# Moving the transposes of the next x back by one step in a fused attention and network kernel

## The reference, cut to what matters

```
emb = silu(sin_emb(timestep)) @ W_ada + b_ada
scale, shift = split(emb)
x = ln(src) * (1 + scale) + shift
q, k, v = x @ Wq + bq, x @ Wk + bk, x @ Wv + bv
scores = q k^T / 4 + attention_bias, masked;  probs = softmax(scores)
x = x + (probs v) @ Wo + bo
```

## Time and profile before

| what | value |
|---|---|
| median of 3 runs | 994.39 us (993.97 to 995.47) |
| profiled execution | 993.79 us, its span 992.0 us |
| attention of the 8 samples | from about 34 to 720 us of the span |
| one sample | 83.5 to 84.3 us |
| steps 14 to 17 of samples 1 to 6 | near 142, 226, 310, 393, 478 and 562 us |

### The profile page before, as it was taken

How to read it: one execution, slowest core, us unless ns; L and a number is a source line. 1 busy time by engine, 2 the same in 40 slices (tenths; PEclk the granted TensorE clock), 3 DMA queues, 4 the chain that set the end, 5 groups by cost and what they waited for, 6 DMA issues and landing times. The chain is left out here.

```text
span 992.0 us, 19948 instructions
## 1 busy us (share of the span) xinstructions
PE 928.4 (94%) x5758; PEld 615.4 (62%) x5838; DVE 749.0 (76%) x2000; ACT 690.1 (70%) x1126; POOL 701.3 (71%) x542
## 2 busy tenths in 40 slices
PE   5879989999998999999999899979999999999996
PEld 5646556655655655665565566545577777777574
DVE  7888788878879787887986878788444765677565
ACT  3577888898788798879878888888644444545333
POOL 1788788788878869878886977877554545567465
PEclk9999999999999999999999999999999999999998
DMA  8988988996996899699689779965111110111101
GB/s 289 326 311 299 381 300 284 340 376 219 333 387 253 294 380 346 234 339 383 238 294 390 282 267 343 368 250 207 64 64 43 43 43 22 43 65 43 43 22 64
DMA packets 127533, 229.96 MB, mean 232 GB/s; under 512 B 6512, under 2 KB 53872, under 8 KB 123632
## 3 DMA queue, kind: packets, MB, share of 16 engines
q1 hardware_dynamic: 127472, 229.26, 63.8%
HBM read 187.30 MB, written 41.94 MB: 231 GB/s over the span
## 5 line engine op out<-in xcount | busy, mean ns | idle before, releaser
L938 ACT ACTIVATE prob<-prob,nmax 128x512 f32<-128x512 f32 x512 | 356.6, 728 | 56.7 <-DVE nmax L760 53.9
L760 DVE CUSTOM_DVE_ANT_0 prob<-s_bank,big 128x512 f32<-128x512 f32 x512 | 338.7, 685 | 63.4 <-POOL big L1102 30.3
L1102 POOL TENSOR_TENSOR big<-big,mterm_early 128x2048 f32<-128x2048 f32 (+2 forms) x88 | 305.7, 3488 | 73.9 <-DMA big<-in_fside_Bx16xSxS 57.6
L591 PEld LDWEIGHTS t_bank<-ident,prob 128*128 128x128 f32 x2048 | 239.8, 141 | 167.5 <-issue 51.7
L591 PE MATMUL t_bank<-ident,prob 128*128 128x128 f32 x2048 | 318.6, 278 | 18.3 <-ACT prob L938 7.1
L945 ACT COPY pt<-t_bank 128x512 f32<-128x512 f32 x312 | 181.0, 583 | 55.4 <-PE t_bank L591 54.2
L769 DVE COPY pt<-t_bank 128x512 f32<-128x512 f32 x200 | 137.3, 687 | 40.0 <-PE t_bank L591 39.8
L579 PE MATMUL s_bank<-stack_k,stack_q 128*128 128x512 bf16 x432 | 165.0, 382 | 2.2 <-DVE nmax L760 1.6
L605 PE MATMUL o_bank<-pt,val 128*32 128x512 f32 x1024 | 122.9, 598 | 3.7 <-issue 1.0
L2201 POOL TENSOR_TENSOR gl<-big,gh 128x512 fp32r<-128x512 f32 x64 | 83.0, 1305 | 49.6 <-DVE gh L1743 49.6
L2052 ACT ACTIVATE big<-bank,late 128x512 f32<-128x512 f32 x62 | 42.6, 689 | 72.6 <-PE bank L1450 69.1
(11 more groups left out here) (247 smaller groups left out, 1454.8 us busy)
## 6 DMA issues: line engine op xcount, KB each, us to landing
big<-in_fside_Bx16xSxS SPq DMA_DIRECT2D x128, 1024.0 KB, 8.0
pieces_dram<-pieces SPq DMA_DIRECT2D x64, 384.0 KB, 7.2
stack_q<-pieces_dram SPq DMA_DIRECT2D x15, 1024.0 KB, 7.8
stack_k<-pieces_dram SPq DMA_DIRECT2D x15, 1024.0 KB, 9.7
pieces_dram<-pieces SPq DMA_DIRECT2D x32, 256.0 KB, 7.4
xin<-in_x SPq DMA_DIRECT2D x8, 512.0 KB, 8.6
x_dram<-x SPq DMA_DIRECT2D x8, 512.0 KB, 2.6
x1r<-x_dram SPq DMA_DIRECT2D x8, 512.0 KB, 4.3
```

Source lines behind the costliest of these rows:

```text
L591: last = pe.transpose(t_bank[n % 2][:, c * P:(c + 1) * P], prob[:, n % NT, c * P:(c + 1) * P], ident[:])
L760: dve.tensor_tensor_reduce(out=prob[:, n % NT, :], in0=s_bank[n % 3][:, :], in1=bias[:, h % NB, t, :], scale=-1.0, scalar=3e38, op0=ALU.ad ...
L938: act.activation(tile, tile, ACT.Exp, bias=nmax[:, n % NT:n % NT + 1], scale=-1.0).then_inc(exped.sem, 1)
L1102: pool.tensor_tensor(bias[:, h % NB, tiles], bias[:, h % NB, tiles], mterm[:, tiles], ALU.add).then_inc(masked.sem, 1)
```

## The change

The two entries of XT in AHEAD go from steps 14 and 15 to steps 15 and 16. VectorE's copies of them, which follow the list, go from steps 15 and 16 to 16 and 17. TAIL with the output projections is as it was. The order within the list and the banks that the uses get are the same.

```diff
 TAIL = [("O", 3, 6, 1), ("C", 0, 7, 1), ("C", 1, 9, 1), ("W", 0, 10, 1), ("W", 1, 12, 1)]
-AHEAD = [("XT", 0, 14, 0), ("XT", 1, 15, 0), ("Q", 0, 21, 0), ("K", 0, 23, 0), ("Q", 1, 28, 0), ("K", 1, 29, 0)]
+AHEAD = [("XT", 0, 15, 0), ("XT", 1, 16, 0), ("Q", 0, 21, 0), ("K", 0, 23, 0), ("Q", 1, 28, 0), ("K", 1, 29, 0)]
```

## The result

The changed kernel takes 996.12 us, the median of 22 runs, beside 994.15 us for the kernel before in 22 runs on the same chips. The ratio is 1.0023, with a 95% interval of 1.0013 to 1.0034: slower by 1.3 to 3.4 us. The profiled execution took 996.44 us (span 994.6), 2.65 more than that of before.

What follows compares the result with a forecast made beforehand. TensorE, busy 94% of the span, was taken as the bound. Samples 1 to 5 +1.70 us, sample 6 -1.33, sample 0 and the last 0: +0.37, put on the 994.39 us median gives 994.8; range 993.4 to 996.9.

Steps and rivals of the forecast that it cites:

- The gate: Turn of step 16 waits for VectorE's copy of step 14; XT 1 falls behind it, weighing 0.34 us later per sample.
- That nothing is caught up later: After steps 14 to 17 TensorE waits only 0.2 us in all (313 to 375 us), so any loss there is kept.
- the term of -1.33 in the sum: Sample 6, behind XT 0: the low clock goes as the longest pause shrinks to 0.93 us; weighing 1.33 us earlier.
- the low clock stays: Rival: a low clock remains in sample 6 or another sample; 6 x 0.34 = +2.04 us, 996.4; chance 0.22.
- a fall in every sample: Rival: frequent short idles make the clock fall in each of samples 1 to 6; +10.4 us, 1004.8; chance 0.04.
- No DMA moves: Whole kernel: the change moves no DMA, only eight transposes on TensorE and two VectorE copies per sample, by one step.
- 1.8 us of cover: XT 1's copy on VectorE ends at 314.99, ACT's high parts read it at 316.78; so its delay costs nothing.
- Sample 0: No output projection ahead and TensorE full there, so the swap costs nothing; bounded by 0 and one 0.34 us.
- Filled for good: Rival: scores of step 18 and turn of step 15 fill XT 0's pause, kept; -4.3 us, 990.1; chance 0.07.
- Absorbed: Rival: VectorE's waits for POOL's masked bias swallow the 0.34; only sample 6 counts, about -1.7 us, 992.7; chance 0.09.

Runs made afterwards that it cites:

- xt_15_15: The kernel before with XT 0 and XT 1 both at step 15: 994.8 us, ratio 1.0008 to the kernel before.
- xt_14_16: The kernel before with XT 1 alone moved, to step 16, XT 0 staying at 14: 999.0 us, ratio 1.0051.
- old_guard8: The kernel before, with POOL's mask add of head 8 waiting until VectorE's low parts are done: 994.6 us, ratio 1.0001.
- first_new: The kernel before with XT at steps 15 and 16 in sample 0 alone: 994.91 us, ratio 1.0020.
- new_guard8: The changed kernel, with POOL's mask add of head 8 waiting until VectorE's low parts are done: 995.49 us, ratio 1.0017 to the kernel before.
- first_old: The changed kernel with XT back at steps 14 and 15 in sample 0 alone: 995.97 us, ratio 1.0013 to the kernel before.
- xt_16_17: The kernel before with XT 0 and XT 1 at steps 16 and 17: 1016.17 us, ratio 1.0248.
- new_take14_act: The changed kernel with step 14 out of DVE_TAKES, so ACT copies that turned tile: 994.58 us, ratio 0.9999 to the kernel before.
- first_new_again: Repeated timing of the kernel before with XT at steps 15 and 16 in sample 0 alone: 994.46 us, ratio 1.0002.

## Why the prediction was right, and where it wasn't

**The gate: right, in place and size.** The turn of step 16 starts 1.87 us behind XT 0 (1.86 in the prediction), the pause for L769 is there at 0.78 in the row (0.94 counted from the end of the issue, as the prediction counted its 0.93), the weighing comes 3.10 us after XT 0 (3.10). XT 0 itself waited 0.00 to 0.48 us and not always 0.51, because the normalisation took 2.43 us in sample 3 where the row of before had 2.75. Four things bear it out: xt_15_15 with 2.66 against 2.65 worked out, xt_14_16 with 3.10, the pair with the late terms at step 20, where the 0.34 is 0.35, and the 2.16 us up to the weighing in samples 1 to 6. That nothing is caught up later held too: from 316 to 378 us TensorE waited 0.2 us in all, as in rows 3, and behind the weighing the samples take the same time in both orders.

**The clock: the term of -1.33 in the sum was wrong.** The one low clock behind XT 0 in sample 6 went into the sum as if each execution had it. Three more profiles have the old order in samples 1 to 6 (old_guard8, first_new and its repetition), and there the clock didn't fall behind XT 0 in any of 18 places, not behind pauses of 1.54 us (first_new, sample 4) and 2.24 us (old_guard8, sample 1) either, so the length of the pause, on which the term was built, doesn't decide it; in xt_14_16, with the same pause ahead of XT 0, it fell in two of six. With the old order itself that is one fall in 24 places, about 0.25 an execution at 1.67 us each; with xt_14_16 it is three in 30, about 0.6. So by this estimate 0.4 to 1 us may be won on average, and not 1.67 each time. In the new order (changed, new_guard8, first_old) none of 18 places fell, which is too few to tell from one in 24. Without the term the sum is 6 x 0.34 = +2.04 us, which lies within the measured 1.3 to 3.4; the number of the rival "the low clock stays" was the better one, if not for its reason. The range of 993.4 to 996.9 holds the 996.12. The rule of the Trainium skill (TensorE: Matmul & The Clock Gate, section A second HAM failure mode), as a fall in every sample, did not come true: none of samples 1 to 6 fell in the changed kernel, although the profile has pauses ahead of the turn of step 15 (0.14), XT 0 (up to 0.48) and the turn of step 16 (0.78) in place of the one ahead of XT 0.

**"No DMA moves": wrong as it stood.** No DMA was put elsewhere in the queue, but SyncE's load of head 8's bias waits for VectorE's bias of step 19, and this came 0.95 us sooner behind the normalisation (4.73 to 3.78) because the copies of XT went behind the biases. The prediction worked out that the bias of step 18 is 0.9 us sooner and didn't ask who waits for its successor. It then gave XT 1's copy 1.8 us of cover towards ACT's high parts, which was right for that wait, and named the cost nothing; the cover that shrank was the other one, between the low parts and POOL's add, from 1.0 to 0.04 us to the end of the pair, and from 1.5 to 0.70 us to the start of the second subtraction, which is what counts. One step further on it fails, with 2.9 us of waiting and some 5 us in all each time (xt_16_17). In the change as made its cost isn't resolved: new_guard8 lies 0.6 us lower, with overlapping intervals, and none of samples 1 to 6 collides in the profile.

**Sample 0: priced at nothing, open between 0 and some 2 us by the timed runs.** The 2.16 us of samples 1 to 6 leave little for it, but its own scatter hides the rest. The transposes there waited for nothing in the two profiles, as said; in xt_14_16, new_take14_act, new_guard8 and first_new_again XT 0 waited 2.05 to 3.38 us for a normalisation of 5.1 to 5.5. What the prediction didn't look at was the low parts of that sample, 5.17 us long before already.

**The other rivals.** Filled for good: excluded, 1.0013 at the least. Absorbed: excluded, it would have been faster by 1.7 us, and behind the weighing the samples take no less time than before.

## What to carry to other kernels

When an engine waits at a place, look for the next gate behind it before filling the pause: here the weight loads of the turn two steps on already waited 0.18 us, and that row said more than the 1.35 us pause itself. Work that lies between two gates hides nothing when it is moved across the second, so the pause has to be taken from what makes the first gate late; moving POOL's mask terms off the normalisation won 0.86%, where moving the transposes lost 0.23%. And when a copy moves behind another instruction, that one becomes early: follow what it releases, through queue and transfer, to the engine that may then run beside something it slows.

## What was not expected of the hardware

VectorE's subtractions with both operands in SBUF take far longer beside POOL's adds. The pair L807 took 1.29 us alone, 2.03 when its start overlapped the end of an add (kernel before, sample 3), and 5.17 when an add of 4.1 us began 0.26 us behind its start, while the add itself went from 4.1 to 4.4 us. The rows look like waiting more than like slow work. In the last case the first subtraction took 0.69 us as ever, and the second took 4.57 and ended 0.55 us behind the add (243.64 and 243.09). In the kernel before the first took 1.43 us and ended 0.56 behind the add of head 7 (318.90 and 318.34). So the price is what is left of the add, and a start some 0.3 us sooner or later decides whether it is paid.

The four operations of the normalisation, L799, with one tensor to read, took 0.41 us each and 1.38 together when alone. Beside L1088, of 0.68 us each, most took 0.78, 2.4 to 3.0 together (3.6 once, in old_guard8); in sample 0 a single one of the four took 4.2 us beside an add, 5.1 to 5.5 together. The Trainium skill (GPSIMD Engine Reference, section Specifications) says that GpSimd shares its SBUF interfaces with VectorE, with contention for VectorE's instructions with two SBUF inputs or in a two-port mode. For L807, with two inputs, the traces agree, with the durations above. L799 is held up too, and no row here tells in which mode it ran.
